# Causal mask of layer 0's score blocks written by ScalarE instead of TensorE, with the blocks regrouped and the dense piece split in two

## The reference, cut to what matters

```python
q, k = _apply_rope(q, cos, sin), _apply_rope(k, cos, sin)
k, v = jnp.repeat(k, rep, axis=1), jnp.repeat(v, rep, axis=1)
scores = jnp.einsum('bhtd,bhsd->bhts', q, k) / math.sqrt(HD)     # HD = 8, T = 512
mask = jnp.triu(jnp.full((T, T), -jnp.inf, dtype=scores.dtype), k=1)
attn = jax.nn.softmax(scores + mask[None, None, :, :], axis=-1)
y = jnp.einsum('bhts,bhsd->bhtd', attn, v)
...
x_up = x @ W_up.T * (Wscale_ug[:INTER] * SCALE)
x_gate = x @ W_gate.T * (Wscale_ug[INTER:] * SCALE)
x = jax.nn.silu(x_gate) * x_up
x = fwht(x * SU_dp) / SCALE
x = x @ W_down.T * (Wscale_dp * SCALE)
```

## Time and profile before

| what | value |
|---|---|
| median of three executions | 1248.34 us |
| the profiled execution, its time | 1250.01 us |
| the profiled execution, its span | 1248.1 us |
| granted TensorE clock, mean over the span | 0.958 of full |
| layer 0's steps with scores of both kinds | from 97.6 us to about 530 us |
| TensorE busy in the span | 1104.5 us (88%) |
| VectorE, ScalarE, GpSimd busy | 690.0, 645.3, 551.0 us |

### The profile page before, as it was taken

The page is one execution under the profiler, slowest core; times in us unless marked ns, Lnnn a source line. Parts: engine busy times, 40 slices in busy tenths (PEclk is TensorE's granted clock), DMA queues, the critical chain, the costliest instruction groups (busy, mean ns, idle before and its releaser), DMA issues. The chain is left out here.

```text
span 1248.1 us, 25068 instructions
## 1 busy us (share of the span) xinstructions
PE 1104.5 (88%) x7537; PEld 659.9 (53%) x7538; DVE 690.0 (55%) x2404; ACT 645.3 (52%) x1340; POOL 551.0 (44%) x524
## 2 busy tenths in 40 slices
PE   6679999999999999987885899888989898888884
PEld 3355666665666666645553455444444454444453
DVE  6486665656566666613395455554545454454526
ACT  4215454545554545563346577656555665566540
POOL 3333131313130000003301587787877787877861
PEclk9899999999999999998898899999989898998987
DMA  7402040214121311020124857857676657866558
GB/s 233 88 23 60 23 98 23 72 19 92 34 59 28 75 38 38 19 70 34 40 75 119 228 111 178 194 96 172 132 179 150 143 110 162 193 144 124 89 114 294
DMA packets 104013, 130.16 MB, mean 104 GB/s; under 512 B 32583, under 2 KB 81991, under 8 KB 103880
## 3 DMA queue, kind: packets, MB, share of 16 engines
q1 hardware_dynamic: 68550, 77.46, 21.9%
q0 software_dynamic: 30720, 47.21, 21.5%
q10 hardware_dynamic: 4616, 3.91, 1.1%
HBM read 89.18 MB, written 38.97 MB: 103 GB/s over the span
## 5 line engine op out<-in xcount | busy, mean ns | idle before, releaser
L689 DVE CUSTOM_DVE_ANT_0 a_masked<-a_ps_s,a_mask 128x512 bf16<-128x512 f32 (+3 forms) x512 | 229.9, 487 | 158.5 <-PE a_ps_s L848 154.7
L1589 POOL DMA_INDIRECT y<-e_y,dst x160 | 255.4, 1596 | 77.0 <-issue 38.7
L605 ACT ACTIVATE a_probs<-a_ps_e 128x512 f32<-128x512 f32 (+1 forms) x384 | 188.2, 527 | 120.8 <-PE a_ps_e L868 119.7
L1812 PE MATMUL e_ps_gu<-e_w_gu,e_xT 128*64 x640 | 217.0, 484 | 1.2 <-issue 1.2
L1812 PE MATMUL e_ps_gu<-e_s_gu,e_xT 128*64 128x352 f32 x640 | 216.9, 484 | 0.0
L187 POOL DMA_INDIRECT yn<-rows,inv x160 | 160.5, 1003 | 119.6 <-DVE inv L1399 59.8
L1837 PE MATMUL e_ps_y<-e_w_d,e_hT 88*64 x640 | 157.7, 390 | 19.7 <-issue 17.4
L1619 ACT ACTIVATE e_y<-e_ps_y,e_weight 128x256 f32<-128x256 f32 x160 | 74.6, 471 | 165.4 <-DMA y<-e_y,dst 133.4
L1837 PE MATMUL e_ps_y<-e_s_d,e_hT 88*64 88x256 f32 x640 | 157.9, 391 | 0.0
L865 PE MATMUL a_ps_e<-a_qT,a_kT 75*128 75x512 bf16 (+3 forms) x512 | 140.8, 303 | 2.1 <-ACT a_probs L605 1.8
L848 PE MATMUL a_ps_s<-a_kT,a_qT 72*128 72x512 bf16 (+3 forms) x512 | 131.3, 300 | 12.3 <-DVE a_headmax L689 11.2
(11 more groups left out here) (236 smaller groups left out, 1819.9 us busy)
## 6 DMA issues: line engine op xcount, KB each, us to landing
e_w_gu<-e_gu SPq DMA_DIRECT2D x64, 352.0 KB
e_w_d<-e_down SPq DMA_DIRECT2D x64, 176.0 KB
a_qT<-qk_parts SPq DMA_DIRECT2D x48, 192.0 KB
y<-a_mask SPq DMA_DIRECT2D x17, 512.0 KB, 5.5
e_w_gu<-y SPq DMA_DIRECT2D x5, 1024.0 KB
qk_parts<-a_stage SPq DMA_DIRECT2D x16, 256.0 KB, 2.6
e_w_d<-y SPq DMA_DIRECT2D x3, 1024.0 KB
yn<-rows,inv POOLq DMA_INDIRECT x160
```

The lines of the kernel that those rows point to most:

```text
L605: nc.scalar.activation(probs[:, i % HKV, UCOL[u]:UCOL[u + 1]], ps_e[:, (i * 3 + u) % 2, 0:w], ACT.Exp, scale=SCALE0).then_inc(exp_done, 1)
L689: ins = V.tensor_tensor_reduce(masked[:, n % 2, c:c + w], ps_s[:, n % 2, c:c + w], mask[:, T - w:T], 1.0, -3e38, ALU.add, ALU.max, headmax ...
L1589: pool.indirect_dma_start(t["y4"], bass.IndirectOffsetOnAxis(dst[:, j:j + 1], 0), y[:, j % NY, :], None, compute_op=ALU.add).then_inc(y_ou ...
L1812: ins = nc.tensor.matmul(ps_gu[r * SEG:(r + 1) * SEG, j % 2, 0:2 * INTER1], xT[:, j // 2 % 2, j % 2, k * P + r * SEG:k * P + (r + 1) * SEG ...
```

## The change

Per head, unit 0 is now the four diagonal blocks (four matmuls of 128 columns, bank 0), unit 1 holds key blocks 0 and 1 against two query blocks each (two of 256, bank 1), unit 2 the remaining two blocks (two of 128, bank 1 too). For heads 1 to 115 the mask is put on bank 0 by a ScalarE copy of `causal`, repeated four times, right after that ScalarE took the exponential of unit 1 of the head before; TensorE's matmuls add to it. For head 0 and the last twelve heads TensorE writes it with one 512-column identity matmul, and the last twelve alternate banks as before. The 128-column tiles of `probs` are placed otherwise so that each unit is one access pattern. Unit 2 now waits for the exponential of unit 1 (the same bank), no longer for that of unit 0. (`DRAIN` in the diff is `HEADS - LAG`, 116.) The dense piece is cut into two halves of two matmuls: the first now stands ahead of `key_scores(i, 2)`, the second where the whole stood.

```diff
+        def mask_written(i):
+            return 1 <= i < DRAIN
+        def score_bank(i, u):
+            return (i * 3 + u) % 2 if i >= DRAIN else min(u, 1)
...
                         act.wait_ge(st_ready, i * 3 + u + 1)
-                        w = UCOL[u + 1] - UCOL[u]
-                        nc.scalar.activation(probs[:, i % HKV, UCOL[u]:UCOL[u + 1]],
-                                             ps_e[:, (i * 3 + u) % 2, 0:w],
+                        nc.scalar.activation(probs_of(i, u), scores_of(i, u),
                                              ACT.Exp, scale=SCALE0).then_inc(exp_done, 1)
+                        if u == 1 and mask_written(i + 1):
+                            act.wait_ge(exp_done, i * 3 + 1)
+                            nc.scalar.activation(ps_e[:, 0, :].rearrange("p (m c) -> p m c", c=P),
+                                                 causal[:, :].rearrange("p (m c) -> p m c", m=1)
+                                                 .to_broadcast([P, TPB, P]), ACT.Copy).then_inc(mask_put, 1)
...
                 x = i * 3 + u
-                if x >= 2:
+                if i == 0 and u < 2:
+                    pe.wait_ge(qkv_copied, EARLY * 2)
+                elif u == 0 and mask_written(i):
+                    pe.wait_ge(mask_put, i)
+                elif u == 2 and i < DRAIN:
+                    pe.wait_ge(exp_done, x)
+                else:
                     pe.wait_ge(exp_done, x - 1)
...
-                for a, c in UNITS[u]:
-                    nc.tensor.matmul(ps_e[:, x % 2, c:c + T - a * P], kT[:, b % 2, g, a * P:(a + 1) * P],
-                                     qT[:, n % NQ, g, a * P:T], start=True, stop=False,
-                                     skip_group_check=True)
-                    ins = nc.tensor.matmul(ps_e[:, x % 2, c:c + P], identb[:, :], causal[:, :],
-                                           start=False, stop=True, skip_group_check=True)
+                if u == 0:
+                    if not mask_written(i):
+                        nc.tensor.matmul(ps_e[:, bank, :].rearrange("p (m c) -> p m c", c=P), identb[:, :],
+                                         causal[:, :].rearrange("p (m c) -> p m c", m=1).to_broadcast([P, TPB, P]),
+                                         start=True, stop=False, skip_group_check=True)
+                    for a in range(TPB):
+                        ins = scores(a, a, a + 1, a, False)
+                elif u == 1:
+                    for a in range(2):
+                        ins = scores(a, a + 1, a + 3, 2 * a, True)
+                else:
+                    far = i % 2
+                    scores(0, 3, 4, 1 - far, True)
+                    ins = scores(2, 3, 4, far, True)
...
                 if y is not None:
                     transpose_y(y)
+                n, c = ffn_at(s)
+                if n is not None:
+                    if c < NI0:
+                        gate_up(n, c, 0)
+                    else:
+                        down(n, (c - NI0) // 2, (c - NI0) % 2, 0)
                 if keys:
                     key_scores(i, 2)
...
                     if c < NI0:
-                        gate_up(n, c)
+                        gate_up(n, c, 1)
                     else:
-                        down(n, (c - NI0) // 2, (c - NI0) % 2)
+                        down(n, (c - NI0) // 2, (c - NI0) % 2, 1)
```

More of the change, by code:

```diff
@@ L877, in values @@
                         pe.wait_ge(y_copied, y)
-                pe.wait_ge(exp_done, (4 * y + 3) * 3 + u + 1)
-                for a, c in UNITS[u]:
+                pe.wait_ge(exp_done, (4 * y + 3) * 3 + 3)
+                for a in VKEYS[u]:
                     for j in range(4):
@@ L883, in values @@
                             v_pad[:, b % NV * TPB + a, 4 * G + j, :],
-                            probs[:, 4 * G + j, UCOL[u] + c:UCOL[u] + c + T - a * P],
+                            key_probs(4 * G + j, a),
                             start=(a == 0), stop=(u == 2), skip_group_check=True)
@@ L912, in transpose_max, with gate_up, down @@
                                     ident[:, :]).then_inc(mT_ready, 1)
-            def gate_up(n, i):
-                if n * NI0 + i:
-                    pe.wait_ge(h_ready, n * NI0 + i)
-                else:
-                    pe.wait_ge(had_copied, 8)
-                if n and i == 0:
-                    pe.wait_ge(added, n * 2)
-                pe.wait_ge(xT_copied, n * 2 + 2)
-                for w in range(2):
-                    for k in range(KD):
-                        ins = nc.tensor.matmul(ps_f[:, w * HALF:(w + 1) * HALF],
-                                               w_gu[:, k, w, i * P:(i + 1) * P], xnT[:, n % NX, k, :],
-                                               start=(k == 0), stop=(k == KD - 1))
-                ins.then_inc(gu_ready, 1)
-            def down(n, i, part):
+            def gate_up(n, i, w):
+                if w == 0:
+                    if n * NI0 + i:
+                        pe.wait_ge(h_ready, n * NI0 + i)
+                    else:
+                        pe.wait_ge(had_copied, 8)
+                    if n and i == 0:
+                        pe.wait_ge(added, n * 2)
+                    pe.wait_ge(xT_copied, n * 2 + 2)
+                for k in range(KD):
+                    ins = nc.tensor.matmul(ps_f[:, w * HALF:(w + 1) * HALF],
+                                           w_gu[:, k, w, i * P:(i + 1) * P], xnT[:, n % NX, k, :],
+                                           start=(k == 0), stop=(k == KD - 1))
+                if w:
+                    ins.then_inc(gu_ready, 1)
+            def down(n, i, part, half):
                 f = n * 2 + i
-                if part == 0:
+                if part == 0 and half == 0:
                     pe.wait_ge(h_ready, (n + 1) * NI0)
@@ L936, in down @@
                         pe.wait_ge(w_ready, 2)
-                for k in range(part * 4, part * 4 + 4):
+                for k in range(part * 4 + half * 2, part * 4 + half * 2 + 2):
                     ins = nc.tensor.matmul(ps_f[:, 0:D], hT[:, k, i * P:(i + 1) * P], w_down[:, k, :],
                                            start=(k == 0), stop=(k == NI0 - 1))
-                if part:
+                if part and half:
                     ins.then_inc(down_ready, 1)
```

40 lines of the change are left out of this document (34 added, 6 removed).

## The result

The changed kernel took 1281.22 us (median of 4 runs, 1276.44 to 1286.21), the kernel before 1251.39 beside it (4 runs, 1246.13 to 1255.03). The ratio is 1.0247, with a 95% interval of 1.0209 to 1.0286. That is 2.5% slower, outside the predicted range. The profiled execution has a span of 1282.3 us instead of 1248.1.

The account below looks back on a forecast made before the run. TensorE was taken as the bound, with the gate wait taking the mask saving: layer 0 +3.2, early steps +3.2, last twelve heads -1.5, in all +4.9 us on 1248.3, so 1253.2 us; range 1240 to 1265.

Parts of the forecast that it names:

- The bound and the mechanism of the steady steps: Layer 0 steps: TensorE bounds them, but removing 0.22 us of mask work uncovers its wait for VectorE's gate.
- The gate step, +0.04 or +0.08: Steps whose dense piece needs a fresh gate: first half waits until 2.25, giving 4.21 us against 4.17 or 4.13.
- Front-end pieces: Transposes or projection, now behind the first half, hide no gate wait: c = 1 +0.42, c = 2 +0.49, c = 10 +0.17 us.
- c = 7 to 11 and the last two blocks: Layer 0 steps: c = 7, 8 +0.04 each, c = 9, 11 -0.22 each, c = 10 +0.17; last two blocks -0.2 us each.
- Mask write and steps without a dense piece: ScalarE's mask copy takes 0.60 us; the four steps c = 12 to 15 of a block, 9.04 us, change by zero in sum.
- Rival (b): ScalarE's mask write takes 1.02 us and delays steps without a dense piece, ten us more in all: 1264; chance 0.07.
- Small matmuls, strided probs: First and last score units' 128-column matmuls run 0.056 to 0.06 us apart; values reading probs at a stride bounds nothing.
- (c): Score units: 128-column matmuls cost at most 0.08 us rather than 0.056, giving 1262 to 1270; chance 0.07 together with (d).
- (d): Values piece: strided reads of probs cost 0.15 us more in half the steps, 8 us, 1261; chance 0.07 together with (c).
- The early steps: First eleven steps, without key scores: third maximum behind the first half makes six VectorE-bound steps 0.63 us longer; +3.2 us together.
- TensorE's clock is no rival: Whole kernel: the clock was dismissed as a rival since TensorE's busy share falls by only some 5%; no chance given.
- The last twelve heads: Heads keeping TensorE's mask: second unit is held less and the last unit is shorter, 0.13 us a head, -1.5 us.

Follow-up runs that it names:

- e4: The changed kernel with VectorE doing the gate (or add) ahead of the first maximum unit; 1242.03 us, ratio 0.9951.
- e1: The changed kernel with the dense piece whole again at its old place, ScalarE's mask and regrouped blocks kept; 1244.51 us against 1247.48 before, ratio 0.998.
- e11: The changed kernel with the front-end pieces (transposes, projection) back ahead of the first dense half; 1266.65 us, ratio 1.0128.
- e3: The changed kernel with the dense piece whole at its old place for s < 12, split later; 1268.61 us, ratio 1.0144.
- e5: e1 with VectorE's gate moved ahead of the first maximum unit; 1263.71 us, ratio 1.0129.
- e8: The changed kernel with the clear of y behind each batch's key loads issued one round later; 1276.84 us, ratio 1.0245.
- e9: e4, but from s = 12 on the dense piece is whole and the third maximum matmul stands behind it; 1243.38 us, ratio 0.9945.
- e10: The changed kernel with four unread 512-column matmuls ahead of the first dense half in early steps from s = 3 on; 1273.74 us, ratio 1.0175.
- e6: The kernel before the change with only VectorE's gate moved ahead of the first maximum unit; 1267.26 us, ratio 1.014.

## Why the prediction was wrong, point by point

**The bound and the mechanism of the steady steps were right.** The gate chain is what the saving runs into. The half starts 2.25 into the step as worked out, and e4 takes the wait away and gains. Of the signs named, TensorE's busy time was to fall by some 25 us in layer 0; it fell by 1.76 a block and by 7 over the span.

**The gate step, +0.04 or +0.08, measured +0.14 and +0.18.** The step of the prediction that failed here is "then half a dense piece, 0.865": it took the rate of a piece whose weight load is hidden, and a first half takes 0.97. With the 56 halves that wait for a gate after 110 us, 0.10 each is 5.6 us. Where there is no wait, c = 0 and c = 11, the split costs 0.10 too (4.26 against 4.16 in e1, 4.03 against 3.94). The rows at 297.88 show the bare load there as well, but whether the wait or the values piece ahead lays it bare, no run separates.

**Front-end pieces.** Predicted c = 1 4.66, c = 2 5.50, c = 10 4.97; measured 4.90, 5.60, 5.15. The mechanism is right and e11 shows it, but c = 1 is 0.24 over: its first half starts at 2.34 instead of 2.25 and takes 0.96 (325.57 to 326.53), its second, behind the transposes, 0.92 (327.21 to 328.13).

**c = 7 to 11 and the last two blocks.** c = 7 4.42 and c = 8 4.53 (+0.14 both, +0.04 predicted); c = 0, 9 and 11 gained 0.13 or 0.14 for the predicted 0.22. The last two blocks became 1.4 and 0.9 us longer instead of 0.2 shorter.

**Mask write and steps without a dense piece.** 0.61 us for the predicted 0.60, the four steps 8.93 against 9.04. Rival (b) is out. The Trainium skill (ScalarE: Activation LUTs, What ACT_TABLE_LOAD costs) gives 186 ns plus 0.833 ns a column for an activation without a pointer operand, by which 512 columns would be 0.61, an estimate; the trace agrees. In their first pass, though, these steps fell to half clock in every kernel with ScalarE's mask (the changed kernel, e1, e3, e4, e5, e8 to e11): c = 15 took 3.89 to 4.33 us there instead of 2.54, which costs about 2 us and was not foreseen.

**Small matmuls, strided probs.** Four score matmuls of 128 columns take 0.22 us from 318.98 on, 0.055 each. The values piece takes 1.07 in both kernels (308.78, 334.70). Rivals (c) and (d) are out: e1 has all of these and is not slower.

**The early steps, "+3.2", measured +12.5, and the sentence behind it: "TensorE's clock is no rival: its busy share falls by some 5%."** This is the step that failed. It judged the clock by the busy share over all of layer 0, and it priced the late third maximum as 0.63 us a step at the full clock. But the clock was already down at 50 us. Before, it was back at 60; in the changed kernel it stayed at 0.50 until 70 and then fell again in every second step, and the steps at the low clock are the long ones. It was not decided by the state ahead of the split: e8 had 0.98 from 40 to 45 us and lost time in the early steps all the same, e9 had 0.67 and was back at 1.00 from 65 on. Nor by the idle time being in one piece: in e4 it is in one piece of 1.2 to 1.3 us and the clock is at 1.00; in the changed kernel the clock is at 1.00 behind the pieces of 1.52 us (75.67, 86.03) and falls at those of 2.21 and 1.82 (80.42, 90.40), but e8 has one of 2.32 (75.83) with the full clock behind it. What decides it stays open. What is shown is that the stretch hangs on the wait for the gate: e3 takes the split away there, e4 makes the wait shorter, and with either the low clock after 65 us and the loss are gone. Which part of the 11 us is the clock's and which VectorE's lateness, no run separates fully; e10 keeps the clock up and wins back 1.5 to 2.6. The Trainium skill (TensorE: Matmul & The Clock Gate, A second HAM failure mode: psum-queue depth-cycling) tells of short idle times between groups of matmuls that let the clock swing between its levels; this trace agrees, with 0.50 and 0.83 where single gaps are at most 2.21 us, and e4 shows that gaps of up to 1.33 did not bring a swing.

**The load waits** had no term. About 5 us of waits in two places against 0.8, and a spell of low clock at each; the blocks that hold them grew by 6.8 and 5.7 us where the others with a front end grew by 1.4 to 2.3.

The account, changed less before at the starts of the blocks: 12.5 to the first key scores, 2 in the first steps without a dense piece, some 12 in seven blocks by the gate and front-end steps, some 8 by load waits and the clock at them: some 35 where the prediction had 6.4 for the early steps and blocks. The last twelve heads gave 0.8 back for the predicted 1.5. So four terms were too small or missing, of which the early one and the gate steps, some 9 each, weigh most. That the direction came out right is owed to the gate wait; the size was not foreseen.

## What to carry to other kernels

When a piece of TensorE's work is split or moved ahead of a wait, look at what stood between two waits of the same step, and follow it to the other engine: here a matmul that VectorE needed came to stand behind the wait, and VectorE was late for the next step. Then ask how long the longest idle piece becomes, and price the steps at the low clock too, above all where the granted clock is down just before. Work that starts behind a wait is priced from a row that also starts behind one, not from the middle of a stream. And before moving work on the engine that waits, look at the order of the engine that is waited for: here two lines on VectorE were worth 39 us, but only in the order of TensorE that could use it (e4 against e5 and e6).

## What the runs showed of the hardware

At the low clock half a dense piece takes 2.07 us for 0.97. The clock came and went in steps of one kernel that do nearly the same work: in the changed kernel's early steps it fell where TensorE had been idle for 2.21 and 1.82 us (80.42, 90.40) and was back in the step behind; in e8 it did not fall at a gap of 2.32 (75.83). The low clock did not keep itself down there. A slow half leaves TensorE no idle time (3.48 us busy of the 3.48 from 80.42 to 83.90), and the next gap is the shorter one, 1.52 us at 86.03.

The first fp32 weight load of a group of matmuls starts with its matmul, not ahead of it, behind a wait and also behind the 32-column values matmuls; such a group takes 0.10 us longer (0.97 against 0.87 for a half piece, 1.83 against 1.73 for a whole one).
